# Experts' products on tokens sorted into tiles of 128, relus on two engines, and another order of slots

## The reference

```python
logits = xt @ Wr + br                                   # (tokens, 8)
# first layer: top 2, gate = softmax over the two; second: top 1, times its softmax probability
h = relu(einsum('td,edh->teh', xt, W1) + b1)            # E = 8 experts
y = einsum('teh,ehd->ted', h, W2) + b2
out = einsum('ted,te->td', y, gate)
x = layernorm(x + out)
```

## Time and profile before

| | us |
|---|---|
| median of 3 runs | 1460.76 |
| lowest, highest | 1448.52, 6079.09 |
| profiled execution, whole | 1460.55 |
| its span | 1458.7 |
| TensorE busy | 1230.4 |
| VectorE busy | 918.5 |
| ScalarE busy | 649.7 |
| GpSimd busy | 170.3 |

### The profile page before, as it was taken

How to read it: one execution, slowest core, us unless ns; L and a number is a source line. 1 busy time by engine, 2 the same in 40 slices (tenths; PEclk the granted TensorE clock), 3 DMA queues, 4 the chain that set the end, 5 groups by cost and what they waited for, 6 DMA issues and landing times.

```text
span 1458.7 us, 27476 instructions
## 1 busy us (share of the span) xinstructions
PE 1230.4 (84%) x10752; PEld 858.3 (59%) x10752; DVE 918.5 (63%) x2432; ACT 649.7 (45%) x1253; POOL 170.3 (12%) x242
## 2 busy tenths in 40 slices
PE   2489999999999999997888998787879986898751
PEld 1356766776676767775555676454556564556530
DVE  2463453536786878877775877975875446544557
ACT  2134345445544554456543446442436643554320
POOL 3221021102200200020000120000030001000011
PEclk9589999999999999998997999997989999999975
DMA  7001110111021102110000010000000000000000
GB/s 273 1 1 44 44 30 17 57 51 52 10 64 51 52 1 73 30 30 1 2 1 1 2 37 1 1 2 1 2 1 2 1 2 2 1 2 1 2 0 29
DMA packets 23143, 35.59 MB, mean 24 GB/s; under 512 B 4568, under 2 KB 12904, under 8 KB 22760
## 3 DMA queue, kind: packets, MB, share of 16 engines
q1 hardware_dynamic: 23016, 33.83, 7.5%
HBM read 32.77 MB, written 1.05 MB: 23 GB/s over the span
## 4 chain that ended last, share of the span: by engine, by line
PE 70%; DVE 13%; ACT 8%; issue 6%; POOL 1%; DVEq 0%; ACTq 0%; POOLq 0%
PE banks L1187 12%; PE banks L1171 11%; PE banks L1925 5%; PE banks L1938 4%; PE banks L1946 3%; DVE arena L2066 2%; ACT XALL L535 2%; PE banks L1967 2%; PE banks L923 2%; PE banks L897 2%; PE banks L545 2%; PE banks L1920 2%; PE banks L661 2%; PE banks L1886 1%; PE banks L937 1%
## 5 line engine op out<-in xcount | busy, mean ns | idle before, releaser
L2066 DVE TENSOR_REDUCE arena<-banks 128x4 f32<-128x1024 f32 x128 | 151.1, 1219 | 106.1 <-PE banks L1902 106.0
L1187 PEld LDWEIGHTS banks<-WE,arena 128*128 128x128 f32 x1536 | 180.0, 192 | 24.4 <-issue 23.3
L1231 ACT ACTIVATE arena<-banks,BC 128x512 f32<-128x512 f32 x192 | 130.5, 688 | 120.2 <-PE banks L1171 119.9
L1187 PE MATMUL banks<-WE,arena 128*128 128x128 f32 x1536 | 182.3, 276 | 0.0
L1171 PE MATMUL banks<-XT,WE 128*128 128x512 f32 x384 | 179.0, 602 | 0.0
L2044 ACT ACTIVATE arena<-banks 128x1024 f32<-128x1024 f32 x128 | 126.4, 1022 | 112.2 <-PE banks L1925 111.5
L1271 DVE SCALAR_TENSOR_TENSOR R<-banks,arena,R 128x128 f32<-128x128 f32 x256 | 71.9, 343 | 111.2 <-PE banks L1187 110.9
L1925 PE MATMUL banks<-arena 32*128 32x256 f32 x1024 | 112.7, 396 | 0.0
L579 ACT COPY arena<-banks 128x512 f32<-128x512 f32 x108 | 61.3, 591 | 115.2 <-PE banks L574 35.8
L1171 PEld LDWEIGHTS banks<-XT,WE 128*128 128x128 f32 x384 | 69.2, 192 | 69.1 <-issue 67.6
L1741 DVE TENSOR_TENSOR arena<-arena 128x512 f32<-128x512 f32 x144 | 100.8, 700 | 3.8
(11 more groups left out here) (305 smaller groups left out, 2149.4 us busy)
## 6 DMA issues: line engine op xcount, KB each, us to landing
WE<-in_weights SPq DMA_DIRECT2D x64, 256.0 KB, 2.9
WE<-in_weights SPq DMA_DIRECT2D x64, 128.0 KB, 2.2
WS<-in_weights SPq DMA_DIRECT2D x1, 2368.0 KB, 13.2
RW<-in_rows SPq DMA_DIRECT2D x1, 1032.0 KB
XALL<-in_x SPq DMA_DIRECT2D x4, 256.0 KB, 10.8
out_dram<-arena SPq DMA_DIRECT2D x4, 256.0 KB, 2.3
WS<-in_weights SPq DMA_DIRECT2D x1, 900.0 KB, 7.9
WS<-in_weights SPq DMA_DIRECT2D x1, 645.0 KB, 8.0
```

The source lines that it names most:

```text
L1187: ins = PE.matmul(v[:, tile(t)], self.HT[:, e % 2, j, tile(t)], self.W[:, (8 * i + e) % RING, 1, j], start=j == 0, stop=j == self.J - 1)
L1231: A.activation(self.HT[:, e % 2, j], psum.view(f"{self.L}.h{i}.{e}.{j}"), ACT.Relu, bias=bcol(self.p + "_b1", e * self.J + j))\
L2066: V.tensor_reduce(big.mx[:, 2 * pair:2 * pair + 2], v, AX.X, ALU.max, negate=True).then_inc(dve.read(f"big.m{i}.{n}.{pair}"), 1)
```

## The change

Each token is now multiplied only with the experts that it chose. The tokens of a chunk are sorted by expert into slots of 128 rows that belong to one expert each. The number of such tiles is fixed at the most that can be needed: TILES = 15 for moe0 (1024 pairs of token and expert) and 11 for moe1 (512). From the chosen experts TensorE counts ranks (`rank_pe`, before16 and ones16), and VectorE makes from them each pair's slot and each tile's expert (`slots_dve`). GpSimd writes the tokens' rows to HBM at their slots, with one indirect DMA for each 128 tokens and choice (8 in moe0, 4 in moe1). SyncE loads the rows back in groups of four tiles (GROUP) and TensorE turns them. Per tile TensorE makes J hidden products of 128x128 and J value products. ScalarE puts the relu on the first half of the hidden units and VectorE on the second. The results go to HBM by SyncE, and GpSimd fetches them with indirect DMAs to the tokens' order; VectorE adds them with the gates.

The expert of a tile is read by SyncE from `EI` into a register, and the load's address depends on it; a third small DMA brings the expert's biases (WB). The regions in HBM are cleared at the start. A slot of rounds holds two tiles in moe0 and three in moe1, and the stages have 18 and 14 slots instead of 11 each. TURNS is another table, of 548 digits instead of 508. The flag of the norm's power is no longer raised where nobody waits for it.

```diff
+PICKS = {"moe0": 2, "moe1": 1}
+TILES = {L: (T * picks + 8 * (P - 1)) // P for L, picks in PICKS.items()}
+GROUP = 4
...
 TURNS = (
-    "00000000000000010010101000101011011010101010112021022010012202021021200121010021101202101201320323031121023012"
...
+    "00000000000000000000000010010011110111100101001010101010001121112102120210110120102020221210210212102121201011"
...
+        slots_in = {(L, i): nc.dram_tensor(f"slots_in_{L}{i}", (TILES[L] * P, D), F32, kind="Internal").ap()
+                    for L in PICKS for i in range(CHUNKS)}
+        slots_out = {(L, i): nc.dram_tensor(f"slots_out_{L}{i}", (TILES[L] * P, D), F32, kind="Internal").ap()
+                     for L in PICKS for i in range(CHUNKS)}
...
-        def load_expert(sp, m, n):
+        def load_expert(sp, m, n, e):

             for j in range(2):
                 a, w = W_AT[EXPERTS[2 * m + j]]
-                a, w = a + n % 8 * (w // 8), w // 8
-                sp.dma_start(WE[m][:, n % RING, j], weights[:, a:a + w]).then_inc(expert_loaded[m][n % RING], 16)
+                sp.dma_start(WE[m][:, n % RING, j], weights[:, bass.ds(e * (w // 8) + a, w // 8)])\
+                    .then_inc(expert_loaded[m][n % RING], 16)
+            a, w = B_AT[f"L{m}_ffn_b1"]
+            with nc.allow_non_contiguous_dma(reason="a column of biases for each 128 hidden units"):
+                sp.dma_start(WB[m][:, n % RING], bcols[:, bass.ds(e * (w // 8) + a, w // 8)])\
+                    .then_inc(expert_loaded[m][n % RING], 16)
...
+                sp.wait_ge(setup_step, 19)
+                for L, i in slots_in:
+                    sp.dma_start(slots_in[L, i].rearrange("(k p) d -> p k d", p=P),
+                                 bc(zeros[:, 0:D], 1, TILES[L])).then_inc(cleared, 16)
...
-                self.hidden_pe(pe, i, 0)
                 pe.wait_ge(sig(L + ".gates"), i + 1)
                 v = psum.take(pe, f"{L}.gT{i}")
                 for t in range(4):
                     ins = PE.transpose(v[0:8, tile(t)], self.GW[:, t, :], ident[:])
                 ins.then_inc(psum.filled(f"{L}.gT{i}"), 1)
                 yield
-                for e in range(8):
-                    if e < 7:
-                        self.hidden_pe(pe, i, e + 1)
-                    self.sum_pe(pe, i, e)
-                    if e < 7:
-                        yield
+                self.rank_pe(pe, i)
+                yield
+                pe.wait_ge(small_loaded, 48)
+                pe.wait_ge(*psum.copied(f"{L}.gT{i}"))
+                v = psum.take(pe, f"{L}.b2{i}")
+                for t in range(4):
+                    ins = PE.matmul(v[:, tile(t)], self.GT[:, tile(t)], B2[:, self.m, :], start=True, stop=True)
+                ins.then_inc(psum.filled(f"{L}.b2{i}"), 1)
+                yield
+                self.turn_pe(pe, i, 0)
+                yield
+                self.turn_pe(pe, i, 1)
+                self.hidden_pe(pe, i, 0)
+                yield
+                for r in self.rounds():
+                    for k in self.a_slot(r):
+                        if k % GROUP == 1 and k // GROUP + 2 < len(self.groups):
+                            self.turn_pe(pe, i, k // GROUP + 2)
+                        if k + 1 < self.N:
+                            self.hidden_pe(pe, i, k + 1)
+                        self.values_pe(pe, i, k)
+                    yield
+                yield
...
+            def turn_pe(self, pe, i, g):
+                L = self.L
+                pe.wait_ge(sig(f"{L}.sorted{min(g, 1)}"), 16 * (i + 1) * (max(len(self.groups) - 1, 1) if g else 1))
+                v = psum.take(pe, f"{L}.sT{i}.{g}")
+                for k in self.groups[g]:
+                    ins = PE.transpose(v[:, tile(k % GROUP)], self.XG[:, k], ident[:])
+                ins.then_inc(psum.filled(f"{L}.sT{i}.{g}"), 1)
...
+            def hidden_pe(self, pe, i, k):
+                n = self.N * i + k
+                pe.wait_ge(expert_loaded[self.m][n % RING], 48 * (n // RING + 1))
+                pe.wait_ge(*psum.copied(f"{self.L}.sT{i}.{k // GROUP}"))
+                for half in range(2):
+                    v = psum.take(pe, f"{self.L}.h{i}.{k}.{half}")
+                    for j in range(self.J // 2):
+                        ins = PE.matmul(v[:, tile(j)], self.W[:, n % RING, 0, self.J // 2 * half + j], self.XS[:, tile(k)],
...
+            def values_pe(self, pe, i, k):
+                L = self.L
+                for half in range(2):
+                    pe.wait_ge(*psum.copied(f"{L}.h{i}.{k}.{half}"))
+                if k % GROUP == 0:
+                    psum.take(pe, f"{L}.y{i}.{k // GROUP}")
+                v = psum.view(f"{L}.y{i}.{k // GROUP}")
                 for j in range(self.J):
-                    v = psum.take(pe, f"{self.L}.h{i}.{e}.{j}")
-                    PE.matmul(v, self.W[:, n % RING, 0, j], XT[:, slot(i)], start=True, stop=True)\
-                        .then_inc(psum.filled(f"{self.L}.h{i}.{e}.{j}"), 1)
-
-            def sum_pe(self, pe, i, e):
+                    ins = PE.matmul(v[:, tile(k % GROUP)], self.HT[:, k % 2, j], self.W[:, (self.N * i + k) % RING, 1, j],
...
+                sp.wait_ge(sig(L + ".experts"), i + 1)
+                for k in range(RING):
+                    self.expert_sp(sp, i, k)
+                yield
+                if i == 0:
+                    sp.wait_ge(cleared, 16 * 2 * CHUNKS)
+                sp.wait_ge(sig(L + ".scattered"), 64 * self.K * (i + 1))
+                for g, tiles in enumerate(self.groups):
+                    rows_of = slots_in[L, i].rearrange("(k p) d -> p k d", p=P)
+                    sp.dma_start(self.XG[:, tiles[0]:tiles[-1] + 1], rows_of[:, tiles[0]:tiles[-1] + 1])\
+                        .then_inc(sig(f"{L}.sorted{min(g, 1)}"), 16)
+                yield
...
+                        if k + RING < self.N:
+                            self.expert_sp(sp, i, k + RING)
+                        if k % GROUP == GROUP - 1 or k == self.N - 1:
+                            self.store_sp(sp, i, k // GROUP)
...
+            def expert_sp(self, sp, i, k):
+                n = self.N * i + k
+                e = sp.value_load(self.EI[0:1, k:k + 1], min_val=0, max_val=7)
+                if n >= RING:
+                    sp.wait_ge(*self.tile_done((n - RING) // self.N, (n - RING) % self.N))
+                load_expert(sp, self.m, n, e)
...
+            def store_sp(self, sp, i, g):
+                L, tiles = self.L, self.groups[g]
+                sp.wait_ge(*psum.copied(f"{L}.y{i}.{g}"))
+                rows_of = slots_out[L, i].rearrange("(k p) d -> p k d", p=P)
+                sp.dma_start(rows_of[:, tiles[0]:tiles[-1] + 1], self.YO[:, tiles[0]:tiles[-1] + 1])\
+                    .then_inc(sig(L + ".stored"), 16)
...
+            def hidden_act(self, act, i, k):
+                n = self.N * i + k
+                act.eng.wait_ge(*psum.made(f"{self.L}.h{i}.{k}.0"))
+                act.eng.wait_ge(expert_loaded[self.m][n % RING], 48 * (n // RING + 1))
+                if k >= 2:
+                    act.eng.wait_ge(*self.tile_done(i, k - 2))
+                for j in range(self.J // 2):
+                    ins = A.activation(self.HT[:, k % 2, j], psum.view(f"{self.L}.h{i}.{k}.0")[:, tile(j)], ACT.Relu,
+                                       bias=WB[self.m][:, n % RING, j:j + 1])
+                    if j < self.J // 2 - 1:
...
+            def hidden_dve(self, dve, i, k):
+                n, half = self.N * i + k, self.J // 2
+                dve.eng.wait_ge(*psum.made(f"{self.L}.h{i}.{k}.1"))
+                dve.eng.wait_ge(expert_loaded[self.m][n % RING], 48 * (n // RING + 1))
+                if k >= 2:
+                    dve.eng.wait_ge(*self.tile_done(i, k - 2))
+                for j in range(half):
+                    ins = V.tensor_scalar(self.HT[:, k % 2, half + j], psum.view(f"{self.L}.h{i}.{k}.1")[:, tile(j)],
...
+            def sum_dve(self, dve, i):
+
+                L, r = self.L, R[:, i]
+                dve.eng.wait_ge(sig(L + ".fetched"), 64 * self.K * (i + 1))
+                dve.eng.wait_ge(*dve.own())
+                for c in range(self.K):
+                    if c:
+                        dve.eng.wait_ge(*dve.own())
+                    for t in range(4):
...
+                pool.eng.wait_ge(sig(L + ".slots"), i + 1)
+                for t in range(4):
+                    for c in range(self.K):
+                        k = self.K * t + c
+                        G.indirect_dma_start(slots_in[L, i], bass.IndirectOffsetOnAxis(ap=self.SLOT[:, k:k + 1], axis=0),
+                                             xc(i)[:, t], None).then_inc(sig(L + ".scattered"), 16)
...
+                pool.eng.wait_ge(sig(L + ".stored"), 16 * len(self.groups) * (i + 1))
+                for t in range(4):
+                    for c in range(self.K):
+                        k = self.K * t + c
```

(3 more changed lines are left out.)

328 lines of the change are left out of this document (206 added, 122 removed).

## The result

| | before | after |
|---|---|---|
| median, us | 1454.64 (4 runs) | 1564.26 (4 runs) |
| lowest, highest | 1442.86, 6079.09 | 1559.63, 1574.84 |
| ratio, 95% interval | | 1.0793 [1.0682, 1.0904] |
| span of the profiled execution | 1458.7 | 1565.4 |
| granted clock over the span | 0.927 | 0.85 |

The change makes the kernel 7.9% slower. The forecast was 1390 us, with a range of 1285 to 1490.

A forecast was written before the change was run, and what follows sets the result against it. TensorE's products were taken to bound the expert stretch. Saving 163 us gave 1296; plus ring 67, HBM 35 and relus 20 made 1418, less 30 a span of 1388, time 1390 us; range 1285 to 1490.

The forecast's parts named there:

- TensorE's work: Expert products removed, 335 us, less 172 us added for tiles, transposes and ranks: 163 us saved, 1,296 us without waits.
- The second estimate: Stretch from 110 to 880 us: 561 us of TensorE work at 82% or 79% busy, giving a span of 1373 to 1399.
- The ring: Three-slot weight ring: TensorE waits for reloads between short tiles, mostly in the second layer; 67 us (37 to 110).
- The reload's price L: Time to reload one weight slot, issues, landing and register steps: taken as 4.5 us, between 3.3 and 6.
- The way through HBM: Scatter, load of sorted rows, store and gather: 22 us missing before transposes, 30 after the last values; 52, reduced to 35.
- rival D: GpSimd's 96 indirect DMAs are slow, near 2.9 us each: 1,511 us; decides from 2.6 us each; chance 0.15.
- The relus: Relus inside a slot, on ScalarE and VectorE both: thin cover costs 0.4 us in each of 48 slots, 20 us (0 to 58).
- The start: Clearing HBM at startup: 23 us more transfer, hidden before chunk 0 scatters at about 100 us; otherwise at most 23 once.
- A quarter of the waits taken off: Discount of 30 from the 122 us of new waits, for idle time already there and in-order engines catching up.
- Rival E: Gaps lower TensorE's clock from 0.96 to 0.85 over 561 us of work, costing 73 us: 1,463 us; chance 0.08.
- Rivals B and C: B: new waits mostly hidden, 1,320 us, chance 0.20. C: VectorE sets the pace, near 80% busy, 1,450 us, chance 0.13.
- The signs: Wrong if: products over 0.24 us a unit, indirect DMAs over 2 us, VectorE ending most TensorE waits, mid-kernel clock under 0.88.

The follow-up runs named there:

- e2: Kernel before, in its own order, with experts 4 to 7 of the first mixture and 3 to 7 of the second left out; 1396.55 us.
- e9: e5 with all relus on ScalarE; 1419.25 us.
- e5: e1 with weights loaded only for chunk 0's first three tiles, tokens and sums taken from SBUF, no scatter, store or gather, clears not waited for; 1446.82 us.
- e1: Changed kernel with the eight clearing DMAs issued at the head of the main block instead of in the setup block; 1537.14 us.
- e7: Kernel before with the new table and 18 and 14 slots, some empty, two experts a slot in the second mixture; 1587.07 us.
- e13: e2's reduced work in the new table of slots, as e7 has it; 1468.10 us.
- e8: e1 with mixture slots stretched over their places in the old table, chunk 3 starting 42 slots later, turned tokens overwriting sorted ones; 1622.17 us.

## Why the prediction was wrong

The measured path from one kernel to the other, each step the difference of two medians (the −58 is 56 against the runs of before that e2 was compared with):

| step | us | from |
|---|---|---|
| fewer products, old order | −58 | e2 − before |
| new table, tiles of 128, ranks, transposes | +23 | e9 − e2 |
| relus shared | +28 | e5 − e9 |
| ring and way through HBM, together | +90 | e1 − e5 |
| clears in the first block | +27 | after − e1 |

**TensorE's work, forecast 163 us less: failed.** The forecast took the whole saving off the span, and the new waits were to be the only price. Measured is 56 for 185 us of products. What the forecast had read was right, that nothing holds up the expert products, and that they fill the time of other stages. It did not draw the conclusion: a product that hides a wait is worth nothing to the span when it goes. The unit of 0.223 us also came from a busy stretch; in the changed kernel the 656 units cover 190 us, 0.289 each, not 146. Even in e9, without the new waits, they cover 171.

**The second estimate, 561 us at 82%: right kind, wrong numbers.** It took the density of the stretch without experts, 82%, as what remains when filler is gone. The stretch came out at 76%, and it held 587 us of work, not 561, although fewer of the other stages' products were in it (2956 instructions for 3432): part of their work had moved behind 880 us. With a density and a duration both taken from rows at the clock of before, it forecast 1373 to 1399 and seemed to confirm the sum, though it was no independent witness.

**The ring, forecast 67 (37 to 110): size right by luck, form wrong.** TensorE's direct waits are 30.2 us, 28 of them, under the lower bound. The reload's price L was taken as 4.5 us. In the 28 waits it was 3.7 in the median (2.9 to 5.5), from SyncE's first step for the reload to the last landing: the 3.6 of the rows and little more. Taking the reloads away brings 73, inside the range, but 49 where the way through HBM is gone too. The direct waits were sized too high, and that a wait costs more than its own length was not foreseen; the two errors cancelled. (The lower bound of L, 3.3, counts three issues where the 3.6 counts two; by the same count it is 2.9.)

**The way through HBM, forecast 35: near in size, not in form.** 41 measured with the ring in place, 17 with it gone. The forecast had TensorE wait for this way; before the transposes of sorted rows, where the sum had 22 us, it waits 6.2. An indirect DMA takes 1.01 us to gather and 0.99 to scatter where 1.1 was taken, so rival D, which needed 2.6, is refuted. The trap behind it (the Trainium skill, SBUF — State Buffer, the "DVE blocks DMA" trap), in which a VectorE operation that has the shared ports keeps GpSimd from writing descriptors, would show as longer gathers beside such operations. Whether the operations below hold these ports no row tells; the trace agrees in direction, in small. Timeline of the changed kernel, GpSimd's gathers and VectorE's operations with two SBUF operands:

```profile
490.66 0.69 DVE L1960 TENSOR_TENSOR arena<-arena 128x512 f32<-128x512 f32 x1
490.74 1.56 POOL L1533 DMA_INDIRECT arena<-slots_out_moe,arena  x1 [7.29 <-DMA slots_out_moe<-arena]
491.38 0.69 DVE L1959 TENSOR_TENSOR arena<-arena 128x512 f32<-128x512 f32 x1
491.99 0.69 DVE L1960 TENSOR_TENSOR arena<-arena 128x512 f32<-128x512 f32 x1
492.61 0.95 POOL L1533 DMA_INDIRECT arena<-slots_out_moe,arena  x1 [0.31 <-issue]
...
495.13 0.94 POOL L1533 DMA_INDIRECT arena<-slots_out_moe,arena  x1 [0.31 <-issue]
...
499.16 1.02 POOL L1533 DMA_INDIRECT arena<-slots_out_moe,arena  x1 [0.30 <-issue]
499.40 0.69 DVE L1959 TENSOR_TENSOR arena<-arena 128x512 f32<-128x512 f32 x1
```

With only small VectorE operations beside it (495.13) a gather takes 0.94 us. Of the gathers that follow another at once, the 26 without a large VectorE operation beside them take 0.94 us in the median, and the 12 that share at least 0.4 us with large ones take 1.02, at most 1.32. A gather that is the first of its series is longer anyway: 0.99 to 1.08 us in three without large operations, 1.11 to 1.57 in three with them, the 1.56 above among them. So the stretch is some 0.5 us at most, far from the 1.5 that the rival needed.

**The relus, forecast 20 (0 to 58): inside the range, too small.** Sharing costs 28 to 38 and TensorE waits 28 us for the two relus. The step named the cause, the queue on VectorE ahead of a tile's relus, and priced it with 0.4 us for each of 48 slots; measured are 10 waits with 6.3 us the longest.

**The start, forecast nothing, or 23 at most: failed.** The forecast counted bytes and a deadline at 100 us. The cost is 27, of another cause: the issues stand in a block whose end all engines wait for. The first wait of the kernel before, 22.6 us, was the same thing and stood in its trace.

**A quarter of the waits taken off, 30: failed.** The ring, HBM and relu steps cost 118 us together against 122 of the sum, so their sum was near before that discount, though only 64 of the 118 are direct waits of TensorE. The discount was put in for idle time that engines would catch up. Here waiting raised the price of what came next.

**Rival E, the clock: happened, with a chance of 0.08.** It said 0.85 and 73 us for the stretch. The clock there is 0.83, and the same other products take 70 us more over the whole kernel. It was treated as an alternative to the waits, but it comes with them. By the rival's own rule the 587 us of the stretch hold about 80 us of it, an estimate (587 x (1 - 0.83/0.96)): priced about right, and left out of the sum. The Trainium skill says that the full clock is for a TensorE that is kept active (TensorE: Matmul & The Clock Gate, "What's actually happening"); the rows agree in direction, with a mixture of 1.2 and 2.4 GHz: 0.927 with 228 us of idle in the kernel before, 0.878 with 309 in e2, 0.850 with 401 in the changed kernel. The clock does not follow idle time alone: e7, with 314, has 0.897.

**Rivals B and C** did not happen: the waits are not hidden, and VectorE is busy 63% in the stretch. It ends more of TensorE's waits than it did (116 us for 67, of them 24.3 at line 1283), yet as a late server, not a full one.

**The signs.** Two of the four signs of being wrong came: products over 0.24 us a unit (0.289), and a clock under 0.88 in the middle (0.83). Indirect DMAs over 2 us, and VectorE ending most of TensorE's waits, did not. TensorE was busy 1164.6 us where 1060 to 1075 was to be seen.

**The table.** The forecast priced the new order only through distances of the new routes. Its effect on everything else, 72 to 134 us on the dense kernel's work, was not in any term, nor was a way to read it from the rows of before. The +23 of the second step is the table at the light dense work, +72 (e13 − e2), and the tiles in its place, −49 (e9 − e13). That is one path only: what the table costs the tiles themselves was not measured, as e8 changes more than the table.

## What to carry to other kernels

When an engine is 94% busy where its removable work lies and 82% where it does not, that work may also be cover: do not count its whole time as saved (here under a third came back, 56 of 185 us), and test it by leaving the work out before building what replaces it. Add the clock to each estimate that makes TensorE idle more, as a cost on all of its other products in the stretch. Keep DMA issues out of a first block that ends for every engine at once. Where a step waits for the later of two engines, look at their queues and not only at their load, and try one engine as well.

## What was not expected of the hardware

- Here the first block waits for its slowest engine: TensorE's first product came at 12.3, 16.3, 22.6 or 45.9 us according to how long SyncE issues DMAs in it. One clearing DMA of 8 took up to 12.6 us to issue.
- The same products outside the mixtures took 860.5 us at a clock of 0.933 and 944.5 at 0.850, 10% more.
- An indirect DMA of 128 rows took GpSimd 0.94 to 1.57 us (1.01 in the mean), with 0.3 us between two.
- A load whose address comes from a register costs SyncE 0.33 us for the issue (0.43 with the fixed address of before) and 0.03 for the move of its address, in the tile's row of the changed kernel (durations min/median/max in ns):

```profile
L370 SPq MOVE WE<-in_weights x208: 3/29/699, 137.3 to 851.5; - x104
L370 SPq DMA_DIRECT2D WE<-in_weights x208: 2/333/1732, 137.4 to 851.5; - x104
```

A single addressed load is thus no dearer than before. A whole tile is: reading its expert into a register, the steps on registers and three issues occupy SyncE for 2.05 us in the median, its waits left out, where two issues had been 0.86. In the second mixture a tile is four units, 1.2 us of TensorE at 0.289. Of the 3.7 us from SyncE's first step to the last landing, 1.2 are up to the third issue and about 2.5 behind it. What a cheaper address would bring was not tried.
